# Gated local-attention mixer on one core: the score mask as a VectorE addition, the maximum subtracted by GpSimd, later lags and a new order inside a slot

## The reference

```python
q, k = l2norm(q) * qs, l2norm(k) * ksc          # 16 heads of 64
q = q*cos*scale + rotate_half(q)*sin*scale      # k with 1/scale
mask = (it < jb) | (it > jb + w) | (jb == -1)   # w = 32, keys: own window and the one before
sim = where(mask, -max, einsum(q, k2) * 8)
x = softmax(sim) @ v2 @ Wo + x
h = layernorm(x) * g + b
x = (a * gelu(gate)) @ W2 + b2 + x              # a, gate = h @ W1 + b1
```

## Time and profile before

| | |
|---|---|
| time, median of 3 runs | 1901.24 us (1900.99 to 1901.6) |
| profiled execution, its own time | 1909.64 us |
| span of the profiled execution | 1907.8 us, mean granted TensorE clock 0.984 |
| share of the span: TensorE, VectorE, ScalarE, GpSimd | 90%, 77%, 57%, 57% |
| DMA | 122.09 MB, 64 GB/s |

### The profile page before, as it was taken

The page is one execution under the profiler, slowest core; times in us unless marked ns, Lnnn a source line. Parts: engine busy times, 40 slices in busy tenths (PEclk is TensorE's granted clock), DMA queues, the critical chain, the costliest instruction groups (busy, mean ns, idle before and its releaser), DMA issues.

```text
span 1907.8 us, 75895 instructions
## 1 busy us (share of the span) xinstructions
PE 1716.4 (90%) x30558; PEld 1209.9 (63%) x30558; DVE 1468.1 (77%) x2727; ACT 1095.4 (57%) x2035; POOL 1088.4 (57%) x970
## 2 busy tenths in 40 slices
PE   5689999999989999999999998999998999999986
PEld 2356666666666666666666666666666666666664
DVE  4688787878877877877887887777887888787764
ACT  2255665656655565656656665656665566566653
POOL 0366665556656655655666666565655655665540
PEclk9699999999999999999999999999999999999999
DMA  2122223222222322222322222222222232222222
GB/s 97 29 78 63 55 57 77 64 66 71 58 48 72 77 69 49 69 57 57 78 63 67 65 62 55 77 64 69 66 55 55 67 77 65 71 58 56 53 54 67
DMA packets 82897, 122.09 MB, mean 64 GB/s; under 512 B 25168, under 2 KB 28752, under 8 KB 82256
## 3 DMA queue, kind: packets, MB, share of 16 engines
q1 hardware_dynamic: 82512, 116.84, 24.4%
HBM read 20.28 MB, written 2.10 MB: 12 GB/s over the span
## 4 chain that ended last, share of the span: by engine, by line
PE 57%; ACT 15%; issue 15%; DVE 11%; ACTq 1%; DMA 0%; DVEq 0%; SPq 0%
PE QKb L450 12%; PE F L573 10%; PE O L510 9%; PE S L498 6%; PE VTb L473 5%; PE S L450 4%; ACT L665 3%; ACT E L665 3%; PE F L596 3%; ACT v_tok L676 3%; PE F L597 2%; PE S L521 2%; PE S L491 2%; ACT KT L659 2%; DVE hid L904 2%
## 5 line engine op out<-in xcount | busy, mean ns | idle before, releaser
L975 POOL TENSOR_TENSOR t<-t 128x512 f32<-128x512 f32 x384 | 488.2, 1271 | 426.1 <-DVE t L835 425.8
L835 DVE TENSOR_TENSOR t<-QKb,table 128x1024 f32<-128x1024 f32 x384 | 469.2, 1222 | 285.0 <-ACT sq L650 281.1
L969 POOL TENSOR_TENSOR t<-t,rn 128x512 f32<-128x512 f32 x384 | 413.7, 1077 | 178.0 <-DVE rn L896 170.9
L450 PE MATMUL QKb<-wq_sb,x_sh 128*128 128x512 f32 x768 | 413.3, 620 | 60.9 <-DVE t L835 51.8
L650 ACT ACTIVATE sq<-QKb 128x512 f32<-128x512 f32 x384 | 229.1, 597 | 332.9 <-PE QKb L450 332.8
L473 PEld LDWEIGHTS VTb<-cst,t 128*128 128x128 f32 x1536 | 193.7, 142 | 204.1 <-issue 202.3
L960 POOL TENSOR_TENSOR E<-E,rs 128x512 f32<-128x512 f32 x192 | 200.2, 1043 | 159.9 <-DVE rs L868 159.9
L510 PE MATMUL O<-PT,V 64*64 64x32 f32 x12288 | 232.2, 221 | 39.6 <-issue 38.1
L682 ACT COPY OT<-O 128x512 f32<-128x512 f32 x192 | 112.5, 586 | 263.8 <-PE O L510 263.8
L510 PEld LDWEIGHTS O<-PT,V 64*64 64x64 f32 x12288 | 205.9, 135 | 62.4 <-issue 43.7
L473 PE MATMUL VTb<-cst,t 128*128 128x128 f32 x1536 | 232.6, 274 | 0.3 <-issue 0.3
(11 more groups left out here) (136 smaller groups left out, 2197.5 us busy)
## 6 DMA issues: line engine op xcount, KB each, us to landing
V<-v_tok SPq DMA_DIRECT2D x1440, 64.0 KB, 2.0
wq_sb<-in_wqkv SPq DMA_DIRECT2D x36, 256.0 KB, 3.1
wo_sb<-in_wo SPq DMA_DIRECT2D x6, 512.0 KB, 3.6
w_sb<-in_w SPq DMA_DIRECT2D x6, 341.0 KB
w_sb<-in_w SPq DMA_DIRECT2D x6, 192.0 KB
y_spill<-OT SPq DMA_DIRECT2D x1, 1024.0 KB, 4.8
V<-y_spill SPq DMA_DIRECT2D x1, 1024.0 KB, 8.0
out<-V SPq DMA_DIRECT2D x4, 256.0 KB, 2.9
```

The costliest lines, as they stand in the source:

```text
L450: return pe.matmul(out_, x_sh[:, pr, P * tile:P * (tile + 1)], wq_sb[:, col:col + 512], start=True, stop=True)
L835: dve.tensor_tensor(t12[:, v, :, :].rearrange("p c (h d) -> p c h d", h=8), QK_ps.rearrange("p (h d) -> p h d", h=8).unsqueeze(1) .to_broa ...
L969: pool.tensor_tensor(w, w, rn[:, vv // 4, 8 * (vv % 4):8 * (vv % 4 + 1)].unsqueeze(2) .to_broadcast([P, 8, DH]), ALU.mult).then_inc(qk_nor ...
L975: pool.tensor_tensor(w, w, t12[:, v, 1, :].rearrange("p (h c d) -> p h c d", h=8, c=2)[:, :, ::-1, :], ALU.add).then_inc(add_done, 1)
```

## The change

- The identity and mask in bfloat16 and the mask product are gone. VectorE adds the mask, broadcast over both banks, as it moves the scores from PSUM to E (semaphore `mask_done`); it then takes the maximum of E in SBUF. GpSimd subtracts it in place (L_SUB = 12).
- What waited for the S banks (transposes of P, V projection) now waits for `mask_done` in place of `sub_done`.
- Exp, normalisation, transposes of P and P·V have lags 13, 14, 16, 17 (12, 13, 14, 15 before). By slot: Exp and sum move to odd slots, normalisation to even ones.
- FFN: Wo in v5, v6, v7, v0; mid v1; mean v3; centring, Square, variance v4; variance copy and Newton v5; broadcast v6; normalisation v0; W1 v1; GELU v2; third chunk, its GELU and hid[0, 1] v3; hid[2] and W2 v4; end v5.
- TensorE: the Q/K projection stands before the first scan piece; the waits of scores and P·V stand before the transposes; broadcast and mean stand at the slot's end.
- ScalarE: GELU of the first chunks stands first in the slot; the FFN's Square behind the eviction of the transposes; mid copies, third GELU and staging ahead of the eviction of O.
- VectorE: Newton stands before t12. GpSimd: scaling and addition first, then subtraction and normalisation.

```diff
-L_S, L_EXP, L_NORM, L_PT, L_PV = 11, 12, 13, 14, 15
-F_WO, F_MID, F_MEAN, F_CENT, F_SQ, F_VAR, F_VCOPY, F_NEWTON = 19, 23, 25, 26, 26, 26, 27, 29
-F_BC, F_XN, F_W1, F_GEL, F_HID, F_W2, F_END = 30, 31, 31, 32, 33, 34, 35
+L_S, L_SUB, L_EXP, L_NORM, L_PT, L_PV = 11, 12, 13, 14, 16, 17
+F_WO, F_MID, F_MEAN, F_CENT, F_SQ, F_VAR, F_VCOPY, F_NEWTON = 21, 25, 27, 28, 28, 28, 29, 29
+F_BC, F_XN, F_W1, F_GEL, F_HID, F_W2, F_END = 30, 32, 33, 34, 35, 36, 37
...
-        ident_bf = sb("ident_bf", [P, P], BF16)
-        mask_bf = sb("mask_bf", [P, 4 * KEYS], BF16)
...
-                    recurrence(in_fill(s, v, 0))
                     if live(g, UNITS):
...
                         project(QK_ps, par, tile, QK_COLS[2 * half + kind]).then_inc(qk_ready, 1)
+                    recurrence(in_fill(s, v, 0))
...
-                        for p in range(2):
-                            pe.matmul(S2[:, p, 0:4 * KEYS], ident_bf[:, :], mask_bf[:, :], start=True, stop=False,
-                                      skip_group_check=True)
...
-                                                   start=False, stop=ct == 3, skip_group_check=True)
+                                                   start=True, stop=True)
...
-                        wait(pe, sub_done, upto(a + 2, QUADS))
+                        wait(pe, mask_done, s_units(s, v))
...
-                        wait(pe, sub_done, s_units(s, v))
+                        wait(pe, mask_done, s_units(s, v))
...
-            dve.tensor_copy(ident_bf[:, :], ident).then_inc(set_dve, 1)
-            dve.tensor_copy(mask_bf[:, :], cst[:, C_MASK:C_MASK + 4 * KEYS]).then_inc(set_dve, 1)
...
                         Sv = S2[:, :, 0:4 * KEYS].rearrange("p b (c k) -> p b c k", k=KEYS)
-                        mv_ = mx[:, k, :].rearrange("p (b c) -> p b c", b=2)
-                        dve.tensor_reduce(mv_, Sv, AX_X, ALU.max).then_inc(max_done, 1)
-                        wait(dve, max_done, a + 1)
+                        Ek = E[:, k, :].rearrange("p (c b k) -> p b c k", c=4, b=2)
                         wait(dve, pt_ready, a - 3)
...
-                        dve.tensor_tensor(E[:, k, :].rearrange("p (c b k) -> p b c k", c=4, b=2), Sv,
-                                          mv_.unsqueeze(3).to_broadcast([P, 2, 4, KEYS]),
-                                          ALU.subtract).then_inc(sub_done, 1)
+                        dve.tensor_tensor(Ek, Sv, cst[:, C_MASK:C_MASK + 4 * KEYS]
+                                          .rearrange("p (c k) -> p c k", k=KEYS).unsqueeze(1)
+                                          .to_broadcast([P, 2, 4, KEYS]), ALU.add).then_inc(mask_done, 1)
+                        wait(dve, mask_done, a + 1)
+                        wait(dve, sub_done, a - 3)
+                        dve.tensor_reduce(mx[:, k, :], E[:, k, :].rearrange("p (c k) -> p c k", k=KEYS), AX_X, ALU.max)\
+                           .then_inc(max_done, 1)
...
+                    a, k, st, pr = quad(s, par, v, L_SUB)
+                    if live(a, QUADS):
+                        wait(pool, max_done, a + 1)
+                        w = E[:, k, :].rearrange("p (c k) -> p c k", k=KEYS)
+                        pool.tensor_tensor(w, w, mx[:, k, :].unsqueeze(2).to_broadcast([P, 8, KEYS]),
+                                           ALU.subtract).then_inc(sub_done, 1)
...
```

More of the change, by code:

```diff
@@ L489, in step @@
                         wait(pe, v_evac, v_units(s, v - 1, L_V))
-                        for p in range(2):
-                            pe.matmul(S2[:, p, 0:4 * KEYS], ident_bf[:, :], mask_bf[:, :], start=True, stop=False,
-                                      skip_group_check=True)
+                    u, vv, st, pr = unit(s, par, v, L_TR)
+                    if live(u, UNITS):
+                        wait(pe, qk_norm, u + 1)
+                        wait(pe, tr_evac, u)
+                        for i in range(4):
+                            mm = pe.transpose(VT_ps[:, P * i:P * (i + 1)], t12[:, vv, 0, P * i:P * (i + 1)], ident)
+                        mm.then_inc(tr_ready, 1)
+                    a, k, st, pr = quad(s, par, v, L_S)
+                    if live(a, QUADS):
                         for ct in range(4):
@@ L555, in step @@
                         mm.then_inc(var_ready, 1)
[L556 to L562, removed]
                     for k in range(QPS):
@@ L584, in step @@
                         ff_w1(f, pr, [0, 1])
+                    f, pr = batch(s, par, v, F_BC)
+                    if f is not None:
+                        wait(pe, diag_done, f + 1)
+                        wait(pe, ff_final, f)
+                        pe.matmul(BANK_BC[:, 0:N], ones[:, :], diag[:, :, :].rearrange("p t q -> p (t q)"),
+                                  start=True, stop=True).then_inc(bc_ready, 1)
                     f, pr = batch(s, par, v, F_HID)
@@ L587, in step @@
                         ff_w1(f, pr, [2])
+                    f, pr = batch(s, par, v, F_MEAN)
+                    if f is not None:
+                        wait(pe, xs_done, 2 * (f + 1))
+                        wait(pe, hid_done, (f - 1) * NCH + 2)
+                        pe.matmul(BANK_MEAN[:, 0:N], mean_w[:, :], xs[:, :], start=True, stop=True)\
+                          .then_inc(mean_ready, 1)
             def ff_w1(f, par, chunks):
@@ L642, in step @@
                     g = s * SLOTS + v
-                    f, pr = batch(s, par, v, F_SQ)
+                    f, pr = batch(s, par, v, F_GEL)
                     if f is not None:
-                        wait(act, cent_done, f + 1)
-                        act.activation(xq[:, :], xc[:, :], ACT.Square).then_inc(xq_done, 1)
+                        gelus(f, pr, [0, 1])
                     if live(g, UNITS):
@@ L660, in step @@
                                  VT_ps.rearrange("p (i q) -> p i q", i=4)).then_inc(tr_evac, 1)
+                    f, pr = batch(s, par, v, F_SQ)
+                    if f is not None:
+                        wait(act, cent_done, f + 1)
+                        act.activation(xq[:, :], xc[:, :], ACT.Square).then_inc(xq_done, 1)
                     a, k, st, pr = quad(s, par, v, L_EXP)
@@ L676, in step @@
                         act.copy(v_tok[:, c // 2, 512 * (c % 2):512 * (c % 2 + 1)], V_ps).then_inc(v_evac, 1)
+                    f, pr = batch(s, par, v, F_MID)
+                    if f is not None:
+                        wait(act, mid_done, f + 1)
+                        act.copy(xs[0:64, :], xm[0:64, pr, :]).then_inc(xs_done, 1)
+                        act.copy(xs[64:P, 1:N], xm[64:P, pr, 0:N - 1]).then_inc(xs_done, 1)
+                    f, pr = batch(s, par, v, F_HID)
+                    if f is not None:
+                        gelus(f, pr, [2])
+                    if v == 5 and live(s + 1, STEPS):
+                        wait(act, qk_ready, s * SLOTS)
+                        wait(act, v_ready, s * (SLOTS // 2))
+                        stage(s + 1, 1 - par)
                     a, k, st, pr = quad(s, par, v, L_PV)
@@ L682, in step @@
                         act.copy(OT[:, pr, 2 * k:2 * k + 2, :], O2[:, :, 0:N]).then_inc(o_evac, 1)
[L683 to L699, removed]
             def gelus(f, par, chunks):
@@ L827, in step @@
                            .then_inc(var_copied, 1)
+                    u, vv, st, pr = unit(s, par, v, L_NEWTON)
+                    f, _ = batch(s, par, v, F_NEWTON)
+                    if vv % 4 == 0 and (live(u, UNITS) or f is not None):
+                        newton(st, vv // 4, u, f)
                     if live(g, UNITS):
@@ L869, in step @@
                     recurrence(in_fill(s, v, 1))
-                    u, vv, st, pr = unit(s, par, v, L_NEWTON)
-                    f, _ = batch(s, par, v, F_NEWTON)
-                    if vv % 4 == 0 and (live(u, UNITS) or f is not None):
-                        newton(st, vv // 4, u, f)
             def newton(st, half, u, f):
```

18 lines of the change are left out of this document (10 added, 8 removed).

## The result

The changed kernel takes 1926.37 us (1925.54 to 1927.19, 4 runs) against 1901.12 for the kernel before: ratio 1.0133, 95% interval 1.0119 to 1.0147. It is slower by 1.3%. The forecast was 1768, faster by 7%, and even its case of a VectorE that becomes the bound stopped at 1845.

The account below looks back on a forecast made before the run. TensorE was taken as the bound, with waits for other engines: a step of 37.37 - 0.88 - 2.45 + 0.75 = 34.8, taken as 34.7, over 46.6 steps plus 8 at the start gave 1768 us, predicted range 1712 to 1845.

Parts of the forecast that it names:

- VectorE becomes the bound: Rival, chance 0.22: GpSimd holds Newton's operations, 2 x 2 holds adding some 3.5 a step on VectorE; 1815 us (1800 to 1845).
- Newton to before t12: VectorE, v1 and v5: hid[2] and the centring no longer wait for Newton, but t12 and the next projection do; covered.
- about 1.7: VectorE in v1: the forecast length in us of the Newton chain, between mid (about 0.4) and t12 (1.2).
- a held first operation: VectorE in v5: Newton with this, finish, variance copy and t12 make about 4.4, against 4.0 plus the issue stall.
- Covered, barely: v1 and v5: TensorE's work, 4.9 in v1 and 4.0 plus the issue stall in v5, hides VectorE's work before t12.
- held until GpSimd's instruction ends: Newton's first operation on VectorE: 170 ns when GpSimd is idle, up to 1035 otherwise.
- the second's price: Newton's second operation on VectorE never met a busy GpSimd (181 to 185 ns); left open, 0 to 1.27 us.
- The chance of a slower kernel: Rival, chance 0.05: four table loads a step, each 1.28, land on the projection loop; a step 39.8, 2005 us.
- The waits of v0, v2, v3: TensorE's waits for other engines, 2.45 a step, lose their causes; a new wait in v2 brings 0.75 back.
- The issue gap in P·V: TensorE in v5, inside the 64 products of P with V: 1.04 a step, left in the forecast.
- the mask product: TensorE: taking it out saves 4 x 0.22 = 0.88 a step, at most 1.24.
- SyncE and the later lags: V moves two slots later, 17.7 a step of issues on SyncE; the later lags cost nothing in steady state.

Follow-up runs that it names:

- sub_first_yields: Changed kernel, GpSimd subtracting ahead of its addition and, in v0 and v4, waiting for the Newton chain ahead of normalisation and scaling: 1770.7 us.
- schedule_alone: Kernel before with the new lags and order, Newton at the slot's end, and mask product, maximum and subtraction as before: 1809.8 us.
- newton_end_sub_first: Changed kernel with Newton back at the end of VectorE's slot and GpSimd's subtraction ahead of its addition, no wait on GpSimd: 1801.8 us.
- gpsimd_yields: Changed kernel, Newton still ahead of t12, GpSimd waiting for the Newton chain before its subtraction in v0 and v4: 1893.4 us.

## Why the prediction was wrong

The step that failed is the fourth of the change, "Newton to before t12", with its "about 1.7" for the chain in v1 and "a held first operation" in v5, and the word "Covered, barely". In the step shown the chain took 4.3 in v1 (981.75 to 986.03) and 3.9 in v5. The cover of v1 was 4.9 of TensorE work less 0.4 + 1.7 + 1.2, so 1.6; the holds were 2.5, and they stood on the loop projection, Square, t12, projection. What is left, 0.9, had nothing to cover it; TensorE's wait in v2 is 1.34.

- *The hold was known, its count wasn't.* The forecast read the earlier trace rows rightly as "held until GpSimd's instruction ends" for the first operation, left the second's price open, and never priced the third. The earlier trace rows had 182 ns for the second because GpSimd stood waiting for Newton itself, in all 93 chains of that stretch, 166 us in all. The change moved Newton into a stretch in which GpSimd has three instructions queued (subtraction, normalisation, scaling), two of them new to that place. The right count was one held operation for each queued instruction. The rival itself says that Newton's later steps would be held too, but its sum took two holds a chain and no more.
- *The rival had the mechanism, not the price.* "VectorE becomes the bound" allowed some 3.5 us of holds a step, and the trace has 353.5 - 152.7 = 201 us of them, 4.2 a step. But it set them against VectorE's idle time, as if any gap could take them. Most of them are paid in series, ahead of t12: 201 us of hold cost 1926.4 - 1770.7 = 156 us of time, and 126 of these are waits of TensorE for t12 (160.1 - 34.0). The chance of a slower kernel was given to the table loads, which cost 25 at most.
- *The rest of the sum held, in part by luck.* Without the holds of the chain (sub_first_yields, which also has another order on GpSimd) the kernel takes 1770.7 us and a step 34.56, for 1768 and 34.7. The waits of v0, v2, v3 went as said: over the run TensorE waits 51.8 us for t12, 23.9 for the V eviction and 11.7 for hid before, and 34.0, none and 2.8 in sub_first_yields; schedule_alone was expected at 1814 by the same sum and came out at 1809.8. The issue gap in P·V was left in and is still there in part (in one step of the changed kernel 0.52 in v7, and 0.36 in the next v5; 26.8 us over the run for 38.1 before).
- *Mis-sized within it:* the mask product, 0.88 a step or 41 us, measured 18.5 in place. That the total fits all the same is luck: other terms were short by about as much. One is known, Newton ahead of t12 without holds, whose gain the sum put at nothing and which is worth 30 by newton_end_sub_first against sub_first_yields.
- SyncE and the later lags cost nothing that a run shows.

What stays open: why Newton ahead of t12 gains 30 us. GpSimd's scaling gets its norms earlier, and VectorE's tail of v1 and v5 is shorter, and no run tells these apart. It isn't the FFN normalisation (L817), which is also held at times: its mean is 689 ns in newton_end_sub_first and 773 in the faster sub_first_yields.

## What to carry to other kernels

Before moving a chain of small SBUF operations on VectorE, look at what GpSimd has queued at its new place, not at the lengths in the old one: a short row there may only say that GpSimd was waiting for it. Count one hold for each queued GpSimd instruction, the first for what is left of it and the others as long as it is, and put them on whatever waits for the chain. If the place is right, let GpSimd wait for the chain by a semaphore, and give it what is urgent first: in this kernel that was worth 156 us of 1926. Then look for what the wait delays: with the subtraction behind it (gpsimd_yields) it was worth 33.

## What the runs showed of the hardware

- VectorE operations with both tensors in SBUF (L889, L892, L894), and the two tensor_scalar operations from SBUF to SBUF (L882 float32, L885 integer), wait for the running GpSimd instruction to end, by the 0.03 to 0.13 us given above. The larger tensor_scalar of the FFN normalisation (L817, 128x256) took 0.41 to 0.42 us where GpSimd was idle and 0.65 to 1.08 where it ran. The mask addition, one operand in PSUM, kept 680 ns, and the maximum and sum, one SBUF input, kept 686 and 676, with GpSimd busy. The Trainium skill (GPSIMD Engine Reference, Key points) names as contending the instructions with two SBUF inputs and those in a two-port mode. The trace agrees on the first kind, by L889, L892 and L894, and no run here shows in what mode L882, L885 and L817 run. It also gives the size: an operation of 0.2 us can last as long as a GpSimd instruction of 1 us.
- It works both ways. In the kernel before, the rstd diagonal (L798, two SBUF tensors) starts 0.04 to 0.05 us ahead of GpSimd's scaling, in all 45 steps between 100 and 1820 us: it keeps its 425 ns, and the scaling takes 1.28 in place of 1.04. In gpsimd_yields the diagonal (L794 there) comes second:

```profile
984.78 1.46 DVE L794 TENSOR_TENSOR xq<-cst,rn 128x256 f32<-128x256 f32 x1
```

```profile
984.67 1.28 POOL L966 TENSOR_TENSOR t<-t 128x512 f32<-128x512 f32 x1
985.91 1.23 POOL L960 TENSOR_TENSOR t<-t,rn 128x512 f32<-128x512 f32 x1
```

It ended at 986.24, after the addition (984.67 + 1.28 = 985.95), and the scaling that started at 985.91, while the diagonal still ran, took 1.23 in place of 1.04.
- A table load took 1.28 us and the next activation followed after 0.02 (in the changed kernel 1001.86 + 1.28 = 1003.14, Exp at 1003.16), as before, with four loads a step for two.
